# Second stage of a transformer block kernel: four quotient buffers, head spreads in four banks, stores by tile, and a new order of its steps

## The reference, cut to what matters

```
h = layernorm(x) * (1 + ca) + sa                    # x: 2 x 4096 x 512
q, k, v = split(h @ w_qkv.T);  q, k = relu(q), relu(k)
vk  = [v; 1] @ k.T                                  # per head of 32
out = (vk @ q)[:-1] / ((vk @ q)[-1] + 1e-15)        # linear attention
x = x + ga * (out @ w_proj.T + b_proj)              # "x1" in the kernel
h = layernorm(x) * (1 + cb) + sb                    # "rows" in the kernel
logits = (h * rsqrt(mean(h*h) + 1e-6) / sqrt(512) * router_scale) @ router_logits
w = softmax(logits);  top 2 of 8 experts, weights renormalised
x = x + gb * sum over the 2 experts of w * ((gelu(h @ Wg) * (h @ Wu)) @ Wd) * scale
```

## Time and profile before

| | |
|---|---|
| time, median of 3 runs | 2202.28 us (2201.35 to 2204.45) |
| the profiled execution's own time | 2204.23 us |
| its span, first to last instruction | 2202.0 us |
| TensorE's mean granted clock | 0.977 |
| TensorE busy | 2082.6 us (95%), 9408 matmuls |
| VectorE, ScalarE, GpSimd busy | 1319.2, 794.9, 801.5 us |
| DMA | 404.89 MB, mean 184 GB/s |

### The profile page before, as it was taken

One profiled execution on the slowest core, in us unless ns is written; L12 is line 12 of the kernel. 1 busy time (PEld: TensorE's weight loads), 2 busy tenths in 40 slices (PEclk: granted clock), 3 DMA queues, 4 the chain that ended last, 5 costly groups with the idle time before them and its releaser, 6 DMA issues.

```text
span 2202.0 us, 42565 instructions
## 1 busy us (share of the span) xinstructions
PE 2082.6 (95%) x9408; PEld 1618.8 (74%) x9409; DVE 1319.2 (60%) x3182; ACT 794.9 (36%) x1493; POOL 801.5 (36%) x618
## 2 busy tenths in 40 slices
PE   7999999999988999983999999999999989999997
PEld 4588887888855666662788888888878778888885
DVE  6555555556358787874555656565565555656554
ACT  3244443444335666651222222222222222222222
POOL 4466655665514667653111111111111111111111
PEclk9999999999989999996999999999999999999999
DMA  7575564556444767676855558558775975865554
GB/s 243 192 244 185 203 204 154 184 203 205 164 153 168 273 218 271 238 265 217 239 129 125 132 123 244 126 127 237 193 181 124 281 175 123 229 140 126 128 109 81
DMA packets 293689, 404.89 MB, mean 184 GB/s; under 512 B 50510, under 2 KB 188750, under 8 KB 285774
## 3 DMA queue, kind: packets, MB, share of 16 engines
q1 hardware_dynamic: 166256, 259.73, 37.0%
q0 software_dynamic: 30000, 72.12, 16.2%
q10 hardware_dynamic: 97200, 70.82, 10.1%
HBM read 210.57 MB, written 191.98 MB: 183 GB/s over the span
## 4 chain that ended last, share of the span: by engine, by line
PE 47%; DMA 3%; issue 1%; SPq 1%; ACTq 1%; DVE 0%; ACT 0%; POOL 0%; DVEq 0%; POOLq 0%
PE bank L1721 47%; DMA act_rows<-hact 2%; ACTq L1033 1%; DMA wbuf<-expert_split 0%; SPq L557 0%; DMA expert_rows<-rows,dest 0%; DMA out_rows<-orow,cur_tok 0%; DVE x_t_lo L1603 0%; DVE act_t_lo L1620 0%; ACT x_t_hi L1015 0%; DVE orow L1648 0%; SPq L555 0%; POOL expert_rows L744 0%; DMA arow<-act_rows 0%; DMA meta<-expert_rows 0%
## 5 line engine op out<-in xcount | busy, mean ns | idle before, releaser
L1721 PE MATMUL bank<-wbuf,x_t_hi 128*128 x2160 | 682.7, 397 | 33.5 <-DVE x_t_lo L1603 30.6
L765 POOL DMA_INDIRECT out_rows<-orow,cur_tok x135 | 209.0, 1548 | 971.8 <-DVE orow L1648 766.3
L1721 PEld LDWEIGHTS bank<-wbuf,x_t_hi 128*128 128x128 f32 x2160 | 409.0, 190 | 132.3 <-issue 35.4
L1721 PE MATMUL bank<-wbuf,x_t_lo 128*128 x1080 | 428.5, 397 | 0.0
L1721 PE MATMUL bank<-wbuf,act_t_hi 128*128 x1080 | 341.6, 397 | 13.4 <-DVE act_t_lo L1620 13.4
L1609 DVE TENSOR_TENSOR hact<-bank,gact 128x512 f32<-128x512 f32 x135 | 93.3, 691 | 379.6 <-PE bank L1721 369.9
L1721 PEld LDWEIGHTS bank<-wbuf,act_t_hi 128*128 128x128 f32 x1080 | 204.0, 189 | 64.8 <-issue 16.8
L1721 PEld LDWEIGHTS bank<-wbuf,x_t_lo 128*128 128x128 f32 x1080 | 204.7, 190 | 48.6
L1721 PE MATMUL bank<-wbuf,act_t_lo 128*128 x540 | 214.5, 397 | 0.0
L1015 ACT ACTIVATE x_t_hi<-bank 128x512 fp32r<-128x512 f32 x135 | 80.8, 599 | 299.2 <-PE bank L1721 285.3
L1039 ACT ACTIVATE act_t_hi<-bank 128x512 fp32r<-128x512 f32 x135 | 80.8, 598 | 289.7 <-DMA arow<-act_rows 202.6
(11 more groups left out here) (218 smaller groups left out, 3835.6 us busy)
## 6 DMA issues: line engine op xcount, KB each, us to landing
wbuf<-expert_split SPq DMA_DIRECT2D x24, 1536.0 KB
xrow<-expert_rows SPq DMA_DIRECT2D x540, 64.0 KB
act_rows<-hact ACTq DMA_DIRECT2D x135, 256.0 KB
arow<-act_rows ACTq DMA_DIRECT2D x540, 64.0 KB
expert_split<-split_hi SPq DMA_DIRECT2D x32, 768.0 KB, 3.6
expert_split<-split_lo SPq DMA_DIRECT2D x32, 768.0 KB, 5.9
xg<-in_x SPq DMA_DIRECT2D x16, 1024.0 KB, 5.4
q_rows<-qf SPq DMA_DIRECT2D x16, 1024.0 KB, 6.7
```

The lines of the kernel that those rows point to most:

```text
L765: pool.indirect_dma_start(out=out, out_offset=bass.IndirectOffsetOnAxis(cur_tok[at][:, 0:1], 0), in_=orow[at % 2][:, :], in_offset=None, c ...
L1721: last = mm(dst, stationary(a, f), moving(b, f), start=(first and k == 0), stop=(k == parts * n - 1))
```

## The change

It touches stage 2 alone, in six edits.

1. `onf` has four buffers, one for each quarter. `divide(g, j)` waits for the `low_on` of the same quarter one group before.
2. From group 1 on the four spreads go into four banks (`RB_OF[1]`: banks 4, 5, `D_B` and `R_B`), and are issued together between projects 1 and 2; the logits and the turned logits wait for the divides that read those banks. The four divides are made together.
3. TensorE: `turn_logits(g - 1)` stands in the middle of project 3, and `denominators(g + 2)` ahead of `rank(g - 1)`.
4. VectorE: `recip(g + 1)` comes first in the turn; the first residual comes before `rms_var`, the second before the router's Newton steps; the steps up to `destinations` come before `centred(g, 3)` and the last Newton steps of the layernorm. ScalarE: the first square of x1 comes before `rms_seed`, `on_hi` 2 and 3 before `logits_out`.
5. The store of `x1` is one transfer of 256 KB for each tile, after its residual, with a semaphore of its own for each tile.
6. GpSimd: the row numbers of group g are written before the scatters of group g - 1, and wait until the scatters of group g - 2 have landed in all four tiles.

```diff
-    onf = [sb(ph2, f"onf{i}", [P, GT], F32) for i in range(2)]
+    onf = [sb(ph2, f"onf{i}", [P, GT], F32) for i in range(HG)]
...
+    RB_OF = [[*RB_B, *RB_B], [*RB_B, D_B, R_B]]
...
# SP, group2
-            sp.wait_ge(s_x1, TPG * (g + 1))
-            sp.dma_start(group_rows(out, g), x1[:, :, :]).then_inc(s_x1st, 16)
+            for t in range(TPG):
+                sp.wait_ge(s_x1, TPG * g + t + 1)
+                sp.dma_start(out[g * GT + t * P:g * GT + (t + 1) * P, :], x1[:, t, :]).then_inc(s_x1st[t], 16)
...
# GpSimd
         def number_rows(g, par):
             if g:
-                wait_apart(pool, s_rowm, 2 * g)
+                pool.wait_ge(s_rowm, 2 * g)
+            for t in range(TPG):
+                at_least(pool, s_scat[t], SCAT * (g - 1))
...
+            number_rows(g, par)
             if g:
                 scatter(g - 1, 1 - par)
-            number_rows(g, par)
...
# ScalarE, group2
+            off_squared(g, 0)
             if before_it:
                 rms_seed(g - 1)
-            off_squared(g, 0)
...
-            if before_it and not more:
-                logits_out(g - 1)
-            square(g, 0, par)
-            if before_it and more:
-                logits_out(g - 1)
-            off_squared(g, 2)
-            square(g, 1, par)
             if more:
                 on_hi(g + 1, 1 - par, 2)
                 on_hi(g + 1, 1 - par, 3)
+            if before_it:
+                logits_out(g - 1)
+            square(g, 0, par)
+            off_squared(g, 2)
+            square(g, 1, par)
...
# VectorE
         def divide(g, par, j):
             dve.wait_ge(s_rb, HG * g + j + 1)
-            at_least(dve, s_onlo, HG * g + j - 1)
-            tt(onf[j % 2][:, :], RB_B[j % 2][:, :], qb[par][:, j, :], ALU.mult).then_inc(s_on, 1)
+            at_least(dve, s_onlo, HG * (g - 1) + j + 1)
+            tt(onf[j][:, :], RB_OF[min(g, 1)][j][:, :], qb[par][:, j, :], ALU.mult).then_inc(s_on, 1)
...
-                at_least(dve, s_x1st, 16 * g)
+            at_least(dve, s_x1st[t], 16 * g)
...
# TensorE
-            at_least(pe, s_on, HG * g + j - 1)
+                at_least(pe, s_on, j - 1)
+            else:
+                pe.wait_ge(s_on, HG * (g - 1) + j + 1)
+            if j == HG - 1:
+                at_least(pe, s_ranku, g - 2)
...
             if a == 0:
-                pe.wait_ge(s_dene, min(g + 3, NG))
+                pe.wait_ge(s_on, HG * min(g + 3, NG))
...
-                spread(g + 1, 0)
-                spread(g + 1, 1)
+                for j in range(HG):
+                    spread(g + 1, j)
...
                 logits(g - 1)
-            spread(g + 1, 2)
-            spread(g + 1, 3)
-            if not before_it:
+                project(g, par, 3, between=lambda: turn_logits(g - 1))
+            else:
                 for a in range(3):
                     project_sums(1, a)
-            if before_it:
-                turn_logits(g - 1)
-            project(g, par, 3)
+                project(g, par, 3)
+            if has(g, 2):
+                denominators(g + 2, par)
             if before_it:
                 rank(g - 1)
-            if has(g, 2):
-                denominators(g + 2, par)
```

More of the change, by code:

```diff
@@ L291, in build @@
         sem("kvp_ready"), sem("kvp_hi_ready"), sem("kvp_lo_ready"), sem("sel_ready"))
-    s_q2, s_x2, s_x1st = sem("q_back"), sem("x_back"), sem("x1_stored")
+    s_q2, s_x2, s_x1st = sem("q_back"), sem("x_back"), [sem(f"x1_tile{t}_stored") for t in range(TPG)]
     s_den, s_aden, s_rec0, s_dene, s_rec, s_rb, s_on = (
@@ L396, in phase2_over @@
             eng.wait_ge(s_scat[t], SCAT * NG)
-        eng.wait_ge(s_x1st, 16 * NG)
+            eng.wait_ge(s_x1st[t], 16 * NG)
         eng.wait_ge(s_zst, 32)
@@ L717, in low_on @@
             pool.wait_ge(s_onhi, HG * g + j + 1)
-            pool.tensor_tensor(on[par][1][:, j, :], onf[j % 2][:, :], f32(on[par][0][:, j, :]), ALU.subtract).then_inc(s_onlo, 1)
+            pool.tensor_tensor(on[par][1][:, j, :], onf[j][:, :], f32(on[par][0][:, j, :]), ALU.subtract).then_inc(s_onlo, 1)
         spread_from = less_sel[:, :].rearrange("p (a n) -> p a n", n=HEAD)
@@ L739, in scatter @@
             pool.wait_ge(s_dest, g + 1)
-            wait_apart(pool, s_rowm, 2 * g + 1)
+            pool.wait_ge(s_rowm, 2 * g + 1)
             for t in range(TPG):
-                wait_apart(pool, s_scat[t], SCAT * g)
+                at_least(pool, s_scat[t], SCAT * g)
                 for k in range(2):
@@ L902, in on_hi @@
             at_least(act, s_y, TPG * (g - 1))
-            act.activation(on[par][0][:, j, :], onf[j % 2][:, :], ACT.Copy).then_inc(s_onhi, 1)
+            act.activation(on[par][0][:, j, :], onf[j][:, :], ACT.Copy).then_inc(s_onhi, 1)
         def off_squared(g, t):
@@ L1443, in group2 @@
             turn.begin(g, ROUTE_STEPS if router else 0)
+            if not last:
+                recip(g + 1)
+            residual(g, 0, par)
             if router:
                 rms_var(g - 1)
-            residual(g, 0, par)
+            residual(g, 1, par)
             if router:
                 rms_seed_squared(g - 1)
-            if not last:
-                recip(g + 1)
-            if router:
                 rms_seed_error()
-            residual(g, 1, par)
             mean(g, 0)
@@ L1459, in group2 @@
             if not last:
-                divide(g + 1, 1 - par, 0)
-                divide(g + 1, 1 - par, 1)
+                for j in range(HG):
+                    divide(g + 1, 1 - par, j)
             var2(g, 0)
@@ L1472, in group2 @@
             residual(g, 2, par)
-            if not last:
-                divide(g + 1, 1 - par, 2)
-                divide(g + 1, 1 - par, 3)
             if router:
@@ L1485, in group2 @@
             now = router and not last
-            centred(g, 2)
             if now:
                 exp_chosen(g - 1)
-            centred(g, 3)
+            centred(g, 2)
             if now:
@@ L1493, in group2 @@
                 scaled()
-            var2(g, 1)
-            if now:
                 renorm_recip()
                 places_chosen()
+                next_places()
+                weights(1 - par)
+                destinations(1 - par)
+            centred(g, 3)
+            var2(g, 1)
             seed_squared(g, 1)
-            if now:
-                weights(1 - par)
             seed_error(1)
-            if now:
-                next_places()
-                destinations(1 - par)
             rstd2_of(1)
@@ L1524, in low_on @@
             dve.wait_ge(s_onhi, j + 1)
-            tt(on[0][1][:, j, :], onf[j % 2][:, :], f32(on[0][0][:, j, :]), ALU.subtract).then_inc(s_onlo, 1)
+            tt(on[0][1][:, j, :], onf[j][:, :], f32(on[0][0][:, j, :]), ALU.subtract).then_inc(s_onlo, 1)
         divide(0, 0, 0)
@@ L1843, in spread @@
                 pe.wait_ge(s_sel, 4 + 2 * NBLK)
-            at_least(pe, s_on, HG * g + j - 1)
+                at_least(pe, s_on, j - 1)
[3 more added lines that the diff above has]
+                at_least(pe, s_ranku, g - 2)
             heads = slice(j * BLK, (j + 1) * BLK)
-            mm(RB_B[j % 2][:, :], less_sel[heads, :], rec[heads, :], start=True, stop=True).then_inc(s_rb, 1)
+            mm(RB_OF[min(g, 1)][j][:, :], less_sel[heads, :], rec[heads, :], start=True, stop=True).then_inc(s_rb, 1)
         def project_sums(b, a):
@@ L1852, in project_sums @@
                 pe.wait_ge(s_mf, HG * b + a // 3)
+                pe.wait_ge(s_on, 2 * HG)
             mm(M_B[b][a][:, :], kv[:, b, a * P:(a + 1) * P], wproj_f[:, a, :], start=True, stop=True).then_inc(s_mp, 1)
@@ L1910, in turn_logits @@
             pe.wait_ge(s_lgt, g + 1)
-            wait_apart(pe, s_ranku, g)
+            at_least(pe, s_ranku, g)
+            pe.wait_ge(s_on, HG * min(g + 3, NG))
             for t in range(TPG):
```

5 lines of the change are left out of this document (2 added, 3 removed).

## The result

The changed kernel takes 2224.03 us (median of 4, 2218.36 to 2238.53), the kernel before 2203.34 beside it (2201.35 to 2204.45). The ratio is 1.0101, 95% interval 1.0063 to 1.0140: about 1% slower, where 19 us less were forecast.

The account below looks back on a forecast made before the run. Stage 2 was held bound by a loop of waits: mask, destinations, scatters, low parts, divides, router. Turns of 21.43 becoming 19.8 gave 21.2 us over 13, less 2 for clock, plus 0.5: 2183.5 us, range 2176 to 2195.

Parts of the forecast that it names:

- TensorE's own work 19.68 us a turn: Stage 2: the turn of 21.32 us less waits of 0.59 for the logits and 1.05 for the mask.
- take 2.12 together instead of 1.06 in two places: Spreads on TensorE after project 1: four issued together were to take 2.12 us, at no cost.
- Four divides, transposes, turned logits inside project 3: Stage 2: divides of 0.69 or less end at about 11, transposes and logits don't wait; the 0.59 us logits wait goes.
- Destinations moved up, 2.5 after the mask: VectorE, mask to destinations: 3.47 us becomes about 2.5, as one centring and some small steps go behind them.
- GpSimd leaves the loop, by a margin of 0.2 to 1 us: GpSimd, stage 2: four low parts end at 18.8 to 19.6, before project 0 needs them at 19.8.
- The second rival: Mask still waits for GpSimd or ScalarE: turn about 20.6 us, gain 10.8 less 1, 2192.5 us; chance 0.22.
- Clock, 2 us: TensorE, middle of stage 2: a turn without slack pays for the 0.99 clock, 3 us at most, 2 taken.
- The third and fourth rivals: Stage 2 scatter landings: rows wait, no change, 2202 us, chance 0.08; or row numbers wait, slower, 2215 us, chance 0.04.
- The rule on 1 MiB: Stores of x1: batching advice, by which four stores take more engine time than one and scatters land later; gain below 19.
- The sum: Whole kernel: 21.2 us over 13 turns, less 2, plus 0.5 at the ends; 19.7 rounded to 19, giving 2183.5 us.

## Why the prediction was wrong

- **TensorE's own work 19.68 us a turn**: mis-sized. It is 18.58; the step "take 2.12 together instead of 1.06 in two places" was wrong, the four take 1.08. The gain from it (1.2 us a turn by the two pairs) was there to be had, and was not in the sum.
- **Four divides, transposes, turned logits inside project 3**: right. The divides take 2.48, the logits' reader doesn't wait, and the router's steps are back to back in 1.9 us.
- **Destinations moved up, 2.5 after the mask**: right in itself (880.52 to 883.01, 2.49). What it is worth hangs on the low parts: with them in one piece, putting it back costs 0.29 us a turn by the profiles; with them apart it gains 1.08, since moving the destinations up brings the low parts nearer to the divides.
- **GpSimd leaves the loop, by a margin of 0.2 to 1 us**: this is the step that failed. I asked only when the low parts would be ready for project 0 and not what VectorE does while they run. I placed them at 13.5 to 19 in TensorE's turn and had VectorE divide until about 11, with centrings and normalisations behind it, and wrote nothing of their meeting. The places themselves came out: scatters 2.34 us into TensorE's turn (859.62 - 857.28), low parts from 12.6 to 17.6, and no project 0 waits for them. But GpSimd stays in the loop, through the VectorE step that the low parts hold for 5.3 us and the mask behind it.
- **The second rival** had the mechanism, from the mask of 1.15 in the earlier trace rows, and the rule that I quoted beside it. Its loop of 20.6 is 2.5 + 0.28 + 11.41 + 6.08 + 0.4; the turn above is 2.49 + 0.28 + 10.26 + 5.02 + 5.6. The term that it had wrong is the last, from the end of the low parts to the end of the mask: I priced 0.4, as if only the router's last steps could be held, and 5.6 us of VectorE's work stood behind the held step. Nor does it have a hold longer than 1.52. In the kernel before a held step got in after one low part each time (the longest holds are 1.1 us), and nothing there showed one that lasted over several. The rule of the Trainium skill, SBUF — State Buffer, "two separate sides", speaks of the whole instruction. The runs go beyond it: one hold can last over four instructions (5.02 us) that stand back to back, though each has a wait of its own for ScalarE, over by then. A wait for the low part before to end lets a step in each time. They also show a form held that has one SBUF tensor as input (`var2`, the 5.44 row above). The same page of the Trainium skill, Who interferes with whom, counts `tensor_scalar` among the forms that can contend.
- **Clock, 2 us**: mis-sized and of the wrong kind. I took it as a small tax on a turn full of TensorE work; it is a cost of the waits, 1.6 us of a project 0 behind a dip, and 1.47 us a turn. With TensorE full, in the kernel with one-column low parts, the clock is 1.00.
- **The third and fourth rivals**: no. GpSimd's wait for landings ahead of the row numbers is in no row of the changed kernel, and with one store in place of the four the turn is the same 23.55. The rule on 1 MiB (the Trainium skill, DMA: Bandwidth & Descriptors, Bandwidth) would have spoken for these rivals; how long a store itself takes, no run here measures.
- **The sum**: 19.7 was rounded to 19, and 2202.3 - 19 is 2183.3 and not 2183.5. Both are under 1 us and change nothing.

What stays open: the profiled turns of the changed kernel give 13 x 2.12 = 27.6 us more than before, the medians 20.7. Only one of its four executions has a trace; more turns of the 22.19 kind in the others would do it, but this was not seen. Stage 3 differs between profiles too: from the last destinations to the end it is 1202.1 us here, 1198.2 before and 1185.3 to 1199.2 in the experiments, none of which touches it; why is not known. And it stays open what decides whether a step gets in between two low parts that stand back to back.

## What to carry to other kernels

Where GpSimd and VectorE both work in SBUF, look up for each GpSimd instruction which VectorE step stands beside it, and give it the steps that read PSUM, or the searches for the largest (MAX8); a small size does not help, as `var2` shows. Don't let GpSimd instructions stand in one piece, though it be faster by itself. A step moved earlier moves what hangs on it, and with full engines that can be onto a worse neighbour: the sum of the waits on the loop that is seen does not tell it. A long wait of TensorE can cost twice, once as a wait and once in the clock behind it, and two loops that feed each other so can have two lengths.

## What the runs showed of the hardware

- Four GpSimd `tensor_tensor` of 128x512 in one piece (5.02 us) hold a VectorE step of 128x2 for 5.3 us, in each of the 13 turns; where each waits for the one before to end (6.11 us for the four) a step is held about 1.5 at a time. Two back to back held a step for both in one run (2.78 us) and let one in between in others (0.56 us for `var2`, of which 0.4 is the hold).
- During low parts, VectorE steps that read PSUM are not held (0.68 and 0.18), nor MAX8 (0.37 for four); held are `scalar_tensor_tensor`, `tensor_tensor` and `tensor_scalar` of SBUF data, from 128x2 to 128x512.
- Four spreads (eight TensorE instructions of 32 rows, each spread from other rows and into another bank) take 1.08 us, two 1.06.
- 1.8 us of matmuls that nobody reads, in each turn, made a kernel 0.9% faster, by keeping the clock at 2.4 GHz where it had fallen to 1.2 behind a wait of 3.5 us. The waits of 1.4 us that were left ahead of the ranks were followed by no dip there, nor was one of 2.76 in the changed kernel; in the kernel with the ranks first and the added matmuls one of six waits of 1.43 was. The length of this one wait does not decide it alone.
